# Expert segments gathered by two engines, the token stage as one ladder of eight chunks, and filler transposes in sliding attention

## The reference, cut to what matters

```python
def _L0_tok_ref(x, emb, W, b):            # token stage: 9 neighbouring rows of the table per token
    idx = jnp.clip(x[..., None] + offsets, 0, INP_SIZE - 1)
    out = jnp.einsum('btkh,ohk->bto', emb[idx], W) + b
...
def _L0_ffn_ref(x, route_id, Wi, bi, Wr, br, Ws, bs, Wo, bo):   # 64 segments of 64 tokens
    h = jax.nn.relu(flat @ Wi.T + bi)
    for l in range(2):
        shared = (jnp.einsum('nd,shd->snh', h, Ws[l]) + bs[l][:, None, :]).mean(axis=0)
        # routed: each segment's own expert, h @ Wr[l, e].T + br[l, e]
        h = jax.nn.relu(shared + routed + h)
    out = h @ Wo.T + bo
...
h = _L0_tok_ref(x, L0_tok_emb, L0_tok_W, L0_tok_b)
h = h + _L0_attn_ref(_layernorm(h), ...)     # linear attention
h = h + _L0_ffn_ref(_layernorm(h), ...)
...
h = h + _L2_attn_ref(_layernorm(h), ...)     # attention to the last 16 positions, 4 heads
```

## Time and profile before

| what | value |
|---|---|
| median of 3 runs | 849.91 us (846.54 to 850.06) |
| profiled execution, its own time | 854.18 us |
| its span | 852.4 us |
| PE busy | 630.7 us, 74% of the span |
| DVE busy | 519.1 us, 61% |
| ACT / POOL busy | 331.4 us / 273.4 us |
| mean granted clock of TensorE | 0.822 |

### The profile page before, as it was taken

One profiled execution on the slowest core, in us unless ns is written; L12 is line 12 of the kernel. 1 busy time (PEld: TensorE's weight loads), 2 busy tenths in 40 slices (PEclk: granted clock), 3 DMA queues, 4 the chain that ended last, 5 costly groups with the idle time before them and its releaser, 6 DMA issues. The chain is left out here.

```text
span 852.4 us, 12948 instructions
## 1 busy us (share of the span) xinstructions
PE 630.7 (74%) x4476; PEld 418.0 (49%) x4476; DVE 519.1 (61%) x1402; ACT 331.4 (39%) x635; POOL 273.4 (32%) x233
## 2 busy tenths in 40 slices
PE   1489755774879378999759999777877652988774
PEld 1446644653767252322347878672322111984653
DVE  0105588653465747567657884428365898744797
ACT  1123201342545223544335553113432974831453
POOL 6431921414030101001157774322001698600420
PEclk9879768686999558989859996566898866999987
DMA  8652231100000010000000000040000000000011
GB/s 275 192 174 69 76 80 45 66 2 1 1 1 0 1 67 1 0 2 1 33 6 12 13 7 12 1 176 0 1 0 31 5 0 0 2 3 1 1 26 25
DMA packets 18781, 30.02 MB, mean 35 GB/s; under 512 B 6434, under 2 KB 15650, under 8 KB 18082
## 3 DMA queue, kind: packets, MB, share of 16 engines
q1 hardware_dynamic: 16162, 19.80, 7.6%
q0 software_dynamic: 2560, 9.44, 3.5%
HBM read 27.25 MB, written 1.05 MB: 33 GB/s over the span
## 5 line engine op out<-in xcount | busy, mean ns | idle before, releaser
L156 POOL TENSOR_TENSOR norm_rstd<-norm_var,minus_half 128x16 f32<-128x16 f32 x16 | 47.4, 2961 | 316.6 <-DVE norm_var L150 316.6
L1247 ACT ACTIVATE m_g<-PS,w_slot 128x512 f32<-128x512 f32 x96 | 60.7, 685 | 73.4 <-PE PS L1301 64.4
L1200 DVE TENSOR_TENSOR m_gw<-m_g,PS 128x512 f32<-128x512 f32 x96 | 61.3, 682 | 41.1 <-PE PS L1309 27.4
L1301 PE MATMUL PS<-m_xT,w_slot 64*128 64x512 f32 x192 | 70.2, 684 | 6.9 <-ACT m_g L1247 6.8
L1325 PE MATMUL PS<-m_gw,w_slot 128*64 128x512 f32 x192 | 57.2, 666 | 0.0
L252 PE MATMUL PS<-w_base,tok_windows 128*128 128x128 f32 x128 | 21.4, 342 | 29.1 <-DMA tok_windows<-in_emb,tok_ids 21.1
L232 POOL DMA_INDIRECT tok_windows<-in_emb,tok_ids x32 | 30.5, 953 | 22.1 <-PE PS L263 9.6
L1309 PE MATMUL PS<-m_gT,m_sel 48*128 48x512 bf16 x96 | 24.1, 418 | 17.8 <-DVE m_gw L1200 12.1
L2047 ACT COPY rat_xf<-PS 64x512 f32<-64x512 f32 x32 | 33.1, 1034 | 10.4 <-PE PS L2103 10.1
L138 DVE BATCH_NORM_STATS2 norm_halves<-H 128x6 f32<-128x64 f32 x256 | 33.8, 209 | 1.3 <-PEq L2637 1.2
L252 PEld LDWEIGHTS PS<-w_base,tok_windows 128*128 128x128 f32 x128 | 19.4, 180 | 30.7 <-issue 13.3
(11 more groups left out here) (341 smaller groups left out, 1669.0 us busy)
## 6 DMA issues: line engine op xcount, KB each, us to landing
rff_routed<-in_routed SPq DMA_DIRECT2D x64, 129.0 KB, 2.1
rat_hf<-in_rat_taps SPq DMA_DIRECT2D x1, 2048.0 KB, 8.2
w_slot<-in_w_rat SPq DMA_DIRECT2D x1, 1589.0 KB, 12.0
w_slot<-in_w_win SPq DMA_DIRECT2D x1, 1378.5 KB, 5.8
w_slot<-in_w_m SPq DMA_DIRECT2D x1, 1329.0 KB, 5.6
w_slot<-in_w_early SPq DMA_DIRECT2D x1, 1092.0 KB
out<-H SPq DMA_DIRECT2D x8, 128.0 KB, 2.2
win_v<-win_v SPq DMA_DIRECT2D x8, 97.5 KB, 2.2
```

The lines of the kernel that those rows point to most:

```text
L156: nc.gpsimd.tensor_tensor(N.rstd[:], N.var[:], C.minus_half[:], ALU.pow).then_inc(S["norm_rstd"], 1)
L1200: nc.vector.tensor_tensor(gw[:, i % 2, half, :], g[:, i % 2, half, :], gate_bank[half], ALU.mult)\
L1247: nc.scalar.activation(g[:, i % 2, half, :], hid_bank[(n - 1) % 3], ACT.Gelu, bias=b1[:, s:s + 1])\
L1301: nc.tensor.matmul(hid_bank[n % 3], w1[lane(half), s, :], pair_of(xT, pair)[lane(half)], start=True, stop=True).then_inc(S["hid_ps"], 1)
```

## The change

1. The token stage loses its two rounds and becomes a ladder with a spacing of 22; every step is issued for one chunk at a time, in the order of chunks. The block that loaded `w_base` ahead of the stage is gone, and its load stands behind that of the ids.
2. The loads of the next stages' weights (`early`, `gate`) wait for chunk 1's gather. SP's loads of segments are those of chunks 4 and 5, behind chunk 5's gather, and of chunks 6 and 7 in linear attention. The segments of chunks 0 and 1 are gathered by POOL in the token stage, behind its 32 gathers of windows and ahead of its rstd, those of chunks 2 and 3 by POOL in linear attention, first of all there. For that the route is loaded to all partitions, and DVE computes row numbers from it once.
3. In linear attention, POOL's rstd of the second half stands behind two chunks' additions and no longer behind four.
4. Sliding attention gets 212 more filler transposes.

```diff
         @block.sync
             sp.dma_start(ids[:], dram["ids"]).then_inc(S["ids"], 16)
+            C.load(sp, "base")
             C.experts.load_route(sp)
+            sp.wait_ge(gathered[1], 16 * G4)
             C.load(sp, "early")
             C.load(sp, "gate")
-            C.experts.load(sp, range(CHUNKS // 2))
+            sp.wait_ge(gathered[5], 16 * G4)
+            C.experts.load(sp, (4, 5))
...
+            C.experts.gather(pool, range(0, CHUNKS // 4))
+            pool.wait_ge(S["const"], 1)
             prepare_next_rstd(nc, pool, C)
...
+            def turn_windows(c, r):
+                w = c % W
+                if r == 0:
+                    pe.wait_ge(gathered[c], 16 * G4)
+                    if c >= W:
+                        pe.wait_ge(S["h_new"], c - W + 1)
...
+            ladder([(34, lambda c: turn_windows(c, 0)), (52, lambda c: turn_windows(c, 1)), (71, turn_tails),
+                    (82, convolve), (117, turn_y)], 22)
...
+            ladder([(39, lambda c: copy_windows(c, 0)), (57, lambda c: copy_windows(c, 1)), (74, copy_tails),
+                    (103, copy_y)], 22)
...
+            def then(n):
+                if n == 215:
+                    v.wait_ge(S["h_new"], W)
+                    prepare_next(nc, v, H, C, True, False)
+                if n == 240:
+                    prepare_next(nc, v, H, C, False, True)
+
+            ladder([(39, lambda c: copy_windows(c, 0)), (57, lambda c: copy_windows(c, 1)), (119, add_bias)], 22, then)
...
 def linear_attention
-            C.experts.load(sp, range(CHUNKS // 2, CHUNKS))
+            C.experts.load(sp, (6, 7))
...
+            C.experts.gather(pool, range(CHUNKS // 4, CHUNKS // 2))
             pool.wait_ge(C.sem("early"), C.count("early"))
-            for c in range(CHUNKS // 2):
+            for c in range(2):
                 C.experts.add_shared(pool, nc.gpsimd.tensor_tensor, c)
                 C.experts.add_bias(nc, C, c)
             norm_rstd(nc, pool, S, C, N, 1)
-            for c in range(CHUNKS // 2, CHUNKS // 2 + 1):
+            for c in range(2, CHUNKS // 2 + 1):
...
+    def gather(self, pool, chunks):
+
+        pool.wait_ge(self.rows_ready, 1)
+        for c in chunks:
+            for j in range(SEGS):
+                at = c * SEGS + j
+                self.nc.gpsimd.indirect_dma_start(
+                    self.routed[:, c, j, :], None, self.dram["routed"],
+                    bass.IndirectOffsetOnAxis(ap=self.rows[:, at:at + 1], axis=0)).then_inc(self.loaded[c], 16)
...
 window_attention, PE
+                    pe.wait_ge(S["mixed"], 2)
+                    rouse(nc, C, PS[3][:, 1, :], 16)
+                if n == 560:
+                    pe.wait_ge(S["h_new"], W + 1)
+                if n % 4 == 0:
+                    if 58 <= n < 228:
+                        rouse(nc, C, PS[3][:, 1, :], 5 if n < 115 else 3 if n < 172 else 1)
+                    if 560 <= n < 660:
+                        rouse(nc, C, PS[0][:, 1, :], 2 if n < 620 else 4)
```

More of the change, by code:

```diff
@@ L106, in rouse, with ladder @@
         nc.tensor.transpose(bank[:, 0:P], C["ident"], C["ident"])
+def ladder(stages, spacing, then=None):
+    for n in range(spacing * (CHUNKS - 1) + max(k for k, _ in stages) + 1):
+        for k, stage in stages:
+            if n >= k and (n - k) % spacing == 0 and (n - k) // spacing < CHUNKS:
+                stage((n - k) // spacing)
+        if then:
+            then(n)
 class NormBuffers:
@@ L199, in token_convolution @@
         S = semaphores(nc, "tok",
[L200 removed]
+                        "const ids windows_read winT_low winT_high winT_ps0 winT_ps1 winT2_low winT2_high "
                         "tailT yT_ps yT y_ps h_new")
@@ new lines, in turn_windows @@
+            def turn_windows(c, r):
[4 more added lines that the diff above has]
+                        pe.wait_ge(S["h_new"], c - W + 1)
+                else:
+                    pe.wait_ge(S["winT_low"], c + 1)
+                    pe.wait_ge(S["winT_high"], c + 1)
+                for k in range(2):
+                    for g in range(G4):
+                        at = (2 * r + k) * P
+                        ins = nc.tensor.transpose(PS[w][:, k, g * P:(g + 1) * P], win[:, c % slots, g, at:at + P], ident)
+                ins.then_inc(S["winT_ps0"] if r == 0 else S["winT_ps1"], 1)
@@ new lines, in turn_tails, with convolve @@
+            def turn_tails(c):
+                w = c % W
+                pe.wait_ge(S["winT2_low"], c + 1)
+                for u in range(U):
+                    tails = PS[w][:, 0, u * P:(u + 1) * P]
+                    nc.tensor.transpose(tails, win[:, c % slots, 2 * u + 1, KC * P - D:], ident)
+                    ins = nc.tensor.transpose(tails[0:D], win[:, c % slots, 2 * u, KC * P:], ident)
+                ins.then_inc(S["windows_read"], 1)
+            def convolve(c):
+                w = c % W
+                pe.wait_ge(S["winT2_high"], c + 1)
+                odd_even = lambda ap: ap.rearrange("p (u h q) -> p h u q", u=U, h=2)
+                y = [PS[w][h * D:(h + 1) * D, 1, 0:U * P] for h in range(2)]
+                for k in range(KC):
+                    for h in range(2):
+                        nc.tensor.matmul(y[h], w_main[:, k, :], odd_even(winT[:, w, k, :])[:, h], start=(k == 0),
+                                         stop=False)
+                pe.wait_ge(S["tailT"], c + 1)
+                nc.tensor.matmul(PS[w][:, 1, 0:U * P], w_tail, tailT[:, w], start=False, stop=True).then_inc(S["yT_ps"], 1)
@@ L284, in _, with turn_y @@
+            def turn_y(c):
+                w = c % W
+                pe.wait_ge(S["yT"], c + 1)
+                for u in range(U):
+                    at = slice(u * P, (u + 1) * P)
+                    ins = nc.tensor.transpose(PS[w][:, 0, at], yT[:, w, at], ident)
+                ins.then_inc(S["y_ps"], 1)
+            ladder([(34, lambda c: turn_windows(c, 0)), (52, lambda c: turn_windows(c, 1)), (71, turn_tails),
+                    (82, convolve), (117, turn_y)], 22)
         @block.scalar
@@ L517, in __init__ @@
         self.nc, self.dram = nc, dram
-        self.route = ctx.enter_context(nc.sbuf_tensor("rff_route", [1, CHUNKS * SEGS], I32))
+        self.route = ctx.enter_context(nc.sbuf_tensor("rff_route", [P, CHUNKS * SEGS], I32))
+        self.rows = ctx.enter_context(nc.sbuf_tensor("rff_rows", [P, CHUNKS // 2 * SEGS], I32))
+        self.rows_ready = ctx.enter_context(nc.semaphore("rff_rows_ready"))
         self.routed = ctx.enter_context(nc.sbuf_tensor("rff_routed", [P, CHUNKS, SEGS, RW], F32))
@@ L1392 @@
 RMS_EPS = 1e-8
-def ladder(stages, spacing, then=None):
-    for n in range(spacing * (CHUNKS - 1) + max(k for k, _ in stages) + 1):
-        for k, stage in stages:
-            if n >= k and (n - k) % spacing == 0 and (n - k) // spacing < CHUNKS:
-                stage((n - k) // spacing)
-        if then:
-            then(n)
 def window_attention(nc, H, PS, C, dram):
@@ L2602, in tower @@
         C.minus_half = minus_half
-        const = ctx.enter_context(nc.semaphore("const"))
         C.out = out
-        with nc.Block() as block:
-            @block.sync
-            def _(sp):
-                C.load(sp, "base")
-            @block.gpsimd
-            def _(pool):
-                nc.gpsimd.memset(minus_half[:], -0.5).then_inc(const, 1)
         stages = [
```

119 lines of the change are left out of this document (35 added, 84 removed).

## The result

The changed kernel takes 882.16 us (median of 4 runs, 881.2 to 885.35) against 849.98 for the kernel before: ratio 1.0394, interval 1.0354 to 1.0433. It is slower by 32 us. I had forecast 840, faster, with 864 as the upper end; the forecast was wrong in its sign. Two later measurements of the same pair gave 1.0376 (1.0353 to 1.0398) and 1.0383 (1.0347 to 1.0420).

The account below looks back on a forecast made before the run. It took the kernel as a chain of stages with barriers, each bound by the engine that ends last. Token stage -15.4, linear attention +8.7 and sliding attention -3 gave -9.7: 849.9 to 840 us, range 826 to 864.

Parts of the forecast that it names:

- What hides the held signals is POOL's longer list: Token stage: it ends with POOL's list at 69.7 us instead of 85.15, -15.4.
- held as before: Rival, chance 0.20: window gathers hold PE's signals until landed; token stage -2, sum +3.7, kernel 854 us.
- the rival that says segments hold too: Chance 0.24: segment gathers also hold signals; token stage +6, linear attention 8.7 + 8, kernel 870 us.
- The late rstd (+8.7): Linear attention: the rstd comes later and DVE's scaling ends at +38.6 instead of +29.9, +8.7 us.
- the upper bound that I named: Linear attention: POOL's additions of chunks 3 and 4 cut in ahead of DVE as well, 8.4 us more.
- A gather's time: Token stage and linear attention: a segment gather takes 1.25 us, like a window gather, both having 128 rows.
- The case by bytes (0.18): Rival, chance 0.18: a segment gather takes 0.55 us; token stage -19, linear attention loses nothing, kernel 828 us.
- Sliding attention (-3): Filler transposes raise TensorE's clock: start +2, end -3, next stage -1.8, sum -3 us.
- the first: Start of sliding attention: fillers delay chunk 0's first step but raise the clock sooner; net +2, between -3 and +5.
- The end part: End of sliding attention: fillers raise the clock from about 541 us on; net -3, between +5 and -8.
- The third: Stage after sliding attention: its 44 fillers start warm and take 4.8 instead of 6.6 us, -1.8.
- my signs for failure: DVE's copies idling over 10 us with a remote releaser, PE's matmuls stretching under POOL's L568, or L568 repeating under 1 us.

Follow-up runs that it names:

- f2_gathers: Kernel before, GpSimd's linear-attention list in the changed order, led by 16 unused gathers of 128 rows x 1032 bytes: 869.81 us, ratio 1.0250.
- f3_narrow: Kernel before, GpSimd's linear-attention list in the changed order, led by 16 unused gathers of 128 rows x 8 bytes: 869.77 us, ratio 1.0228.
- f4_few_rows: Kernel before, GpSimd's linear-attention list in the changed order, led by 16 unused gathers of 32 rows x 1032 bytes: 870.20 us, ratio 1.0238.
- j2_one_by_one: Kernel before with 8 unused gathers ending GpSimd's linear-attention list, each issued when the one before has landed, chip with the hold: 849.36 us, ratio 1.0003.
- e3_segments: Kernel before with its two rounds, segments fetched as in the changed kernel, no unused transposes: 884.54 us, ratio 1.0411.
- i3_ladder_24: Kernel before with the eight-chunk sequence, unused transposes and all segments by SyncE (24 transfers in the token stage), chip with the hold: 846.50 us, ratio 0.9955.
- i1_after: The changed kernel again, nothing altered, on a third chip, which has the hold: 881.68 us, token stage 100.0.
- f1_busy: Kernel before, GpSimd's linear-attention list in the changed order, led by seven small unused powers, no gather: 866.68 us, ratio 1.0190.
- i2_late: Kernel before with 16 unused gathers behind GpSimd's additions in linear attention, chip with the hold: 860.00 us, ratio 1.0122.
- e1_fillers: Kernel before with only the 212 unused transposes in sliding attention: 842.72 us, ratio 0.9928.
- h3_direct: Kernel before with 16 plain GpSimd transfers behind its additions in linear attention, chip without the hold: 836.33 us, ratio 1.0009.
- h2_late: Kernel before with 16 unused gathers behind GpSimd's additions in linear attention, chip without the hold: 836.77 us, ratio 1.0011.

## Why the prediction was wrong, by its own steps

**"What hides the held signals is POOL's longer list" (the token stage's -15.4) failed.** It took the hold to end with the windows and PE's 40 us of work to fit under POOL's list. The hold goes on through the segment gathers, because it comes with gathers issued in a row, whatever they carry (f2_gathers, f3_narrow, f4_few_rows, j2_one_by_one). The term measured +16.5 in the two profiles and about +20 against the usual token stage. e3_segments has +18 of it without the sequence of eight chunks, i3_ladder_24 has 79.5 us with the sequence and no segment gather. So the segment gathers are the cause, at the full length of their list (20.5 us, i1_after less i3_ladder_24), and the sequence alone is worth 1 to 3 us. Nor was chunk 1's copy in the earlier trace rows due at 20.60, as I wrote: PE had been done since 19.44 (17.47 + 1.97 in the trace), so its signal too was late. What I read as the stage's reserve (85.15 down to 69.7) is what the hold costs before: the chip without it runs the code of before in 68.3 to 69.9 us. My bound for "held as before" was -2; the rival that says segments hold too gave +6 and was right in kind. It was too small since it put 8 us of loss on 20 us of gathers; the rows of the changed kernel show 11.70 and 13.65 us of idling in and around those 20 us, with one instruction of DVE between them.

**The late rstd (+8.7) was mis-sized.** f1_busy has it without gathers: +17.2. The wait for the rstd was foreseen. But the scaling ran beside POOL's additions and took 9.31 us instead of 1.41, and an addition to H was locked out behind it. That is the upper bound that I named, 8.4 us more, and set aside. In the changed kernel the loss comes by another way, with DVE 11 us late by the hold, POOL ahead, and 8 us of lock; f2_gathers, which has both, costs 3 us more than f1_busy. The two overlap: the hold alone costs 10 us (i2_late) and the list alone 17, together 20. My rival added 8.7 and 8 and had 17.

The Trainium skill, in "SBUF — State Buffer", section "Who interferes with whom", has DVE with two SBUF inputs and a GpSimd instruction that reads SBUF lock each other out for a whole instruction. The 3.93 and 4.15 us of the additions to H agree. The same line of DVE took 0.42 us at 98.43 in f1_busy, in the midst of seven small powers of POOL that read SBUF; as in the earlier trace rows, the rule doesn't hold for these.

**A gather's time** goes neither by bytes nor mainly by rows: I took 1.25 us, and it was 1.25 to 1.26. The case by bytes (0.18) is out: f3_narrow's rows of 8 bytes take 0.95 us too. (128 rows of 1032 bytes are 132 KB and not 129, so that case had to be 0.56 us.) The Trainium skill, in "DMA: Bandwidth & Descriptors", section "SWDGE vs HWDGE vs iDMA", says that software on GpSimd computes one descriptor pair per DMA operation. If each row is such an operation, as I read it, the 0.87 us for 32 rows beside 0.95 for 128 say that little of an issue's time here goes by their number.

**Sliding attention (-3) was right in kind and too small**: 4.2 and 2.0 us, 6 in the whole kernel (e1_fillers). Of its three terms the first held: +2 for the start, and +2.5 came. The end part is the mis-sized one: -3, and -7.0 came; the clock was down there for 13.7 us, where I had counted on some 22. The third was right by luck: -1.8 because the next stage's 44 fillers would start warm and take 4.8 us. The stage got 2.0 shorter, but the 44 took what they took before (6.58), since the clock fell once more under them; PE's timeline in the changed kernel:

```profile
597.09 6.66 PE L106 MATMUL PS<-w_base 128*128 128x128 f32 x44 [1.76 <-PEq L2670]
```

**The sum**: -15.4 + 8.7 - 3 = -9.7 against +20 + 20 - 6. Of my signs for failure, one came: copies that idle over 10 us with a remote releaser.

What a chip without the hold makes of the changed kernel was not measured, since the two repeats met a chip with it; nor were GpSimd's plain transfers (h3_direct) measured on a chip with the hold. What it is in the chip that holds PE's signals and SP, and why one chip of three doesn't show it, is open; nothing here says whether it is the chip or something else that ran beside the kernel there. The end of the hold was not tried by an experiment of its own: in linear attention the last late signal arrives 1.3 to 2.8 us behind the last gather's landing (i2_late, f2_gathers, f3_narrow, f4_few_rows), but single ones get through earlier, as ACT's copy at 127.78 did. My reading before, that all run again when the last gather has landed, is thus only about right.

Of the kernels here the best on chips with the hold is the one before with the unused transposes alone: 842.7 us, against 849.5. With the sequence and SP's segments it is 846.5; its token stage is 1 us shorter (3 us on the chip without the hold), but its linear attention 4 us longer, probably as chunk 3's addition comes behind the rstd; that was not tested alone.

## What to carry to other kernels

Idle time with a remote releaser beside a row of gathers isn't slack that a longer list can hide: ask what the hold depends on before adding to it, and measure one more gather where nothing else changes. A work list that is moved ahead of a short instruction on POOL costs twice, by the wait and by the long additions that now run beside DVE's two-input instructions; take the upper bound when they come in a row. Price each part alone: the one that helped here (6 us) was hidden under two that lost 40.

## What the runs showed of the hardware that I had not expected

- While gathers are issued 1.25 us apart, PE's signals come late and keep other engines idle for up to 12.2 us at a time (f3_narrow), and SP issues 7 transfers in 18.0 us instead of 15 in 22.4, on two of three chips. The signals of DVE and ACT to PE are not held (0.05 us at most). 16 gathers cost 10 us by themselves (i2_late), on the third chip nothing (h2_late), and before runs 837.2 there against 849.4 to 850.3. Row size (8 or 1032 bytes) and number of rows (32 or 128) change nothing, a gap of 3.1 us between gathers takes the hold away (j2_one_by_one).
- A gather's issue takes 0.95 us and 0.30 between two for rows of 2304, 1032 and 8 bytes.
- The same program's token stage took between 80.2 and 84.7 us in nine executions with the hold, so one profile of a held stage is good to some 4 us only.
